# Attention's softmax sum in an audio tower: the second tree level moves from GpSimd to VectorE

## The reference, cut to what matters

```python
logits = jnp.einsum('avhd,bthd->abhvt', k, q) / math.sqrt(HEAD_DIM)   # a: 64 videos, v: 12 frames, h: 2 heads
weights = jax.nn.softmax(logits, axis=3)                              # over the 12 frames
attn = jnp.einsum('avhd,abhvt->abhtd', v, weights)
attn = attn.transpose(0, 1, 3, 2, 4).reshape(V, T, Nw, EMBED)
attn = attn.mean(axis=0)                                              # over the videos
o = attn @ Wo.T + bo
```

## Time and profile before

| | us |
|---|---|
| median of 3 runs | 2392.04 |
| lowest and highest | 2386.63, 2396.46 |
| the profiled execution's own time | 2387.96 |
| its span | 2386.1 |
| PE busy | 2052.9 (86%) |
| DVE busy | 1563.6 (66%) |
| ACT busy | 1079.6 (45%) |
| POOL busy | 769.3 (32%) |
| the 96 chunks of attention, in the span | about 1145 to 1635 |

### The profile page before, as it was taken

The page is one execution under the profiler, slowest core; times in us unless marked ns, Lnnn a source line. Parts: engine busy times, 40 slices in busy tenths (PEclk is TensorE's granted clock), DMA queues, the critical chain, the costliest instruction groups (busy, mean ns, idle before and its releaser), DMA issues. The chain is left out here.

```text
span 2386.1 us, 54761 instructions
## 1 busy us (share of the span) xinstructions
PE 2052.9 (86%) x20986; PEld 1812.3 (76%) x20986; DVE 1563.6 (66%) x3984; ACT 1079.6 (45%) x2700; POOL 769.3 (32%) x730
## 2 busy tenths in 40 slices
PE   6599989998726776786899999994999999999998
PEld 5497778786615676686677777773999999999998
DVE  4745665654743653556699999996666676676664
ACT  4433333422614453452666666662444444444443
POOL 0002222200055424520577777774121121121120
PEclk9899999999858897898999999997999999999999
DMA  7100100100311101100000000000000000000000
GB/s 180 37 1 12 15 11 12 15 1 2 111 42 35 30 20 35 36 16 1 3 3 3 3 3 3 3 3 1 8 8 7 13 7 7 13 7 7 13 7 14
DMA packets 80356, 44.52 MB, mean 19 GB/s; under 512 B 45800, under 2 KB 74024, under 8 KB 79752
## 3 DMA queue, kind: packets, MB, share of 16 engines
q1 hardware_dynamic: 74248, 29.53, 5.4%
q0 software_dynamic: 5888, 12.07, 1.9%
HBM read 27.20 MB, written 14.38 MB: 17 GB/s over the span
## 5 line engine op out<-in xcount | busy, mean ns | idle before, releaser
L2103 ACT ACTIVATE w<-banks,b 128x384 f32<-128x384 f32 (+1 forms) x512 | 259.5, 572 | 392.9 <-PE banks L2177 392.9
L2159 PE MATMUL banks<-w,w 128*128 128x128 f32 (+1 forms) x3072 | 364.1, 275 | 0.0
L2159 PEld LDWEIGHTS banks<-w,w 128*128 128x128 f32 (+1 forms) x3072 | 350.4, 189 | 9.1 <-issue 8.7
L1694 PE MATMUL banks<-qT,w 64*64 64x128 f32 x4608 | 272.2, 271 | 14.9 <-DVE eb L1597 12.3
L1702 PE MATMUL banks<-eb,w 64*64 64x128 f32 x4608 | 272.4, 271 | 0.7 <-DVE eb L1597 0.7
L1694 PEld LDWEIGHTS banks<-qT,w 64*64 64x64 f32 x4608 | 249.3, 133 | 29.8 <-DVE eb L1597 17.0
L2004 DVE SCALAR_TENSOR_TENSOR h<-banks,t_wt,h 128x128 f32 (+3 forms) x672 | 183.9, 343 | 115.1 <-PE banks L2159 112.4
L1702 PEld LDWEIGHTS banks<-eb,w 64*64 64x64 f32 x4608 | 249.2, 133 | 1.3 <-DVE eb L1597 1.1
L1237 POOL DMA_INDIRECT xg<-xs,rowu x184 | 179.2, 974 | 152.3 <-PE banks L1388 90.4
L1662 POOL TENSOR_TENSOR t<-eb 128x768 f32<-128x768 f32 x96 | 175.9, 1832 | 135.8 <-ACT eb L1642 123.7
L1597 DVE TENSOR_TENSOR eb<-eb,rd 128x1536 f32<-128x1536 f32 x96 | 211.7, 2205 | 1.6 <-ACT rd L1651 1.6
(11 more groups left out here) (309 smaller groups left out, 4354.4 us busy)
## 6 DMA issues: line engine op xcount, KB each, us to landing
out<-h SPq DMA_DIRECT2D x16, 320.0 KB
xs<-r_xl SPq DMA_DIRECT2D x16, 192.0 KB, 2.9
h<-in_xT SPq DMA_DIRECT2D x4, 750.0 KB, 15.0
h<-in_xT SPq DMA_DIRECT2D x4, 749.0 KB, 17.9
xg<-xs,rowu POOLq DMA_INDIRECT x184
xs<-r_xl SPq DMA_DIRECT2D x16, 128.0 KB
blocks<-NT SPq DMA_DIRECT2D x24, 48.0 KB, 1.9
D<-blocks SPq DMA_DIRECT2D x24, 48.0 KB, 2.0
```

Of the source, the lines that this page charges most:

```text
L1694: last = nc.tensor.matmul(lbanks(n)[place(n, hd), v, :], k.Kt[half(hd), v, :], qT[half(hd), n // NC % 2, (n % NC) * P:(n % NC + 1) * P], s ...
L2103: nc.scalar.activation(gb[u % 2][:, f, s * GW:s * GW + NFREE[s]], k.ps[:, order.bank(n), 0:NFREE[s]], ACT.Relu, bias=k.b1_1[:, 2 * e + f:2 ...
L2159: last = nc.tensor.matmul(k.psf[0:n, o:o + P], gb[u % 2][:, f, c * P:c * P + n], k.w2_1[:, 2 * e + f, :], start=(f == 0), stop=(f == 1))
```

## The change

`t1` gets a second buffer. POOL keeps only the first add, alternating between the buffers, and counts `tree` once a chunk. The second add moves to DVE, ahead of `den`, with a new semaphore `folded` on which DVE waits before it reads `t2`, and on which POOL waits before it writes a buffer of `t1` again.

```diff
-        t1 = sb("t1", [P, 6, P])
+        t1 = sb("t1", [P, 2, 6, P])
...
-        counted, logged = sem("ao_counted"), sem("logged")
+        counted, logged, folded = sem("ao_counted"), sem("logged"), sem("folded")
...
                     w = n - 2
                     if 0 <= w < NCH:
-                        dve.wait_ge(tree, 2 * w + 2)
+                        dve.wait_ge(tree, w + 1)
+                        nc.vector.tensor_tensor(t2[:], t1[:, w % 2, 0:3], t1[:, w % 2, 3:6], ALU.add).then_inc(folded, 1)
+                        dve.wait_ge(folded, w + 1)
                         if w >= 2:
                             dve.wait_ge(logged, w - 1)
                         nc.vector.tensor_reduce(den[:, w % 2, :], t2[:].rearrange("p v t -> p t v"), AX_X,
...
                 for n in range(NCH):
                     e = eb[:, n % 4]
                     pool.wait_ge(e_ready, 3 * n + 3)
-                    if n:
-                        pool.wait_ge(tree, 2 * n)
-                    nc.gpsimd.tensor_tensor(t1[:], e[:, 0:6], e[:, 6:12], ALU.add).then_inc(tree, 1)
-                    pool.wait_ge(tree, 2 * n + 1)
-                    if n:
-                        pool.wait_ge(summed, n)
-                    nc.gpsimd.tensor_tensor(t2[:], t1[:, 0:3], t1[:, 3:6], ALU.add).then_inc(tree, 1)
+                    if n >= 2:
+                        pool.wait_ge(folded, n - 1)
+                    nc.gpsimd.tensor_tensor(t1[:, n % 2], e[:, 0:6], e[:, 6:12], ALU.add).then_inc(tree, 1)
```

## The result

| | before | with the change |
|---|---|---|
| median, lowest, highest of 20 runs, us | 2391.8, 2382.9, 2409.3 | 2384.7, 2373.0, 2392.5 |
| ratio to before, 95% interval | | 0.9967 (0.9953 to 0.9982) |
| from the first maximum of attention to the first instruction behind it | 490.97 us | 484.67 us |

A forecast was written before the change was run, and what follows sets the result against it. PE and DVE are near full, with PE's own cycle as the floor. Saving 0.31 us a cycle, times 14, gives 4.3; the ends give 0.7; 5.0 off 2392.04 makes 2387.0 us, range 2378 to 2397.

The forecast's parts named there:

- floor of 29.23 us a cycle: PE alone could run six attention iterations in 29.23 us against 30.08, a ceiling near 12 us over 14 steady cycles.
- The fold: 0.55 and 0.03 of gap: The add moved to DVE takes 0.55 us plus 0.03 waiting for its semaphore: a slot of 0.58, bounds 0.47 and 0.70.
- The new wait behind ACT: 0.54: PE's turn of x waits 0.54 us for ACT's output copy, once a cycle; before, the wait for the multiply covered it.
- C: Third of six PE iterations in a cycle, with a turn of x; its first matmul waited for DVE's multiply before.
- The sum: 4.3 + 0.7: 0.31 us less a cycle, times 14, gives 4.3 us; both ends of attention give 0.7; together 5.0 us off.
- 0.1 us of slot costs 0.2 a cycle: Each 0.1 us more on the fold's DVE slot comes twice before den, so costs 0.2 us a cycle.
- The multiply's mean at 2.05 to 2.1: Sign that the forecast is right: DVE's multiply in attention averages 2.05 to 2.1 us.
- The walk's 0.5 and 0.8 us: Walking one cycle, the multiply stands still 0.5, 0.8, 0.5 and 0.8 us in the last four of six iterations.
- Rival 1, all 12 us: No new wait behind ACT appears, so all 12 us come back: 12.6 us off, 2379.4 us; chance 0.15.
- Rival 3: The fold starts after POOL's add and stands until it ends: 25 us more, 2417 us; chance 0.15.
- B: Second of six PE iterations in a cycle, plain; the fold was expected to start 0.47 us before POOL's add there.
- Without the second buffer POOL would wait for the fold: In attention, the bigger t1 is on no path and costs nothing; with one buffer POOL would wait for the fold.

The follow-up runs named there:

- experiment 3: The change with ACT's three normalisations moved ahead of the logarithm; attention stretch 478.24 us, 6.4 below the change, ratio 0.9934 to before.
- experiment 8: The change without the fold: POOL writes a token's six frames adjacent in t1, one DVE reduce sums them; stretch 476.83 and 476.93 us, ratio 0.9933 to before.
- experiment 9: The change with POOL's add cut to one token of 128, other sums left out; stretch 476.84 us, 7.8 below the change, ratio 0.9938 to before.
- experiment 4: The kernel before, with only ACT's normalisations moved ahead of the logarithm; stretch 490.98 us against 490.97 before, ratio 0.9998.
- experiment 5: Repeat runs of the change, 484.66 us, ratio 0.9989 to before, and of the change with ACT's normalisations ahead of the logarithm, 478.28 us, ratio 0.9944.
- experiment 6: The change with one DVE reduce of six frames in place of fold and den; stretch 497.14 us, 12.5 over the change, ratio 1.0025 to before.
- experiment 7: The change with one six-frame reduce for fold and den, and ACT's normalisations ahead of the logarithm; stretch 488.51 us, 3.8 over the change, ratio 1.0000.
- experiment 10: The change with the fold done twice, each with its wait; stretch 571.11 us, 86 over the change, ratio 1.0339 to before.
- experiment 2: The change with only one buffer for t1; stretch 484.93 us, 0.26 over the change, ratio 0.9976 to before.
- experiment 1: The kernel before with only the second buffer of t1, both adds left on POOL; stretch 488.67 us, 2.3 less than before, ratio 0.9992.

## Why the prediction was right, point by point

- *PE bounds, with a floor of 29.23 us a cycle.* Right. Experiments 3, 8 and 9 reach 29.22, 29.24 and 29.23 by three different ways and go no lower, though 9 frees 29 us of DVE.
- *The fold: 0.55 and 0.03 of gap.* 0.54 and 0.03 to 0.04. The Trainium skill's sentence ("VectorE: DVE Perf Modes", section "The DRAIN you can't avoid") that a semaphore costs nothing is about eight copies and does not fit these rows: a DVE instruction that waits for nothing starts 0.08 to 0.09 us before the record ahead ends (the maximum behind `den`, the fold behind `bn_stats`), and `den`, which waits for the fold's semaphore, 0.03 to 0.04 after it. No run has the fold and `den` without that semaphore.
- *The new wait behind ACT: 0.54.* 0.47 measured, in C and nowhere else. The 0.12 that I put between ACT's copy and the turn was an upper bound, and the trace has 0.06: the copy ends at 1300.72 and the turn starts at 1300.78. Experiments 3 and 4 show that ACT's order is its cause, and that the old wait covered it.
- *The sum: 4.3 + 0.7.* The cycle gave 0.39 and not 0.31, so 5.5 in 14 cycles; the other 0.8 of the 6.3 us is what remains for the ends, where 0.7 were an estimate. At the start it does not come as I had put it: `den` of the first chunk is 0.48 us earlier (7.74 us behind the first maximum, 8.22 before), but the first multiply stands beside POOL's next add and ends 13.57 us behind that maximum in both kernels; the gain comes in the iterations after it. The term that was mis-sized is the wait in C, by 0.07 us. That the measured medians and ratio came near (7.1 and 7.9 us) is in part luck, as experiment 5 shows.
- *0.1 us of slot costs 0.2 a cycle.* The cycle of experiment 6 fits it, at a slot 0.33 longer. It is no longer of use where DVE sets the cycle (experiments 7 and 10).
- *The multiply's mean at 2.05 to 2.1.* 2.057. The walk's 0.5 and 0.8 us are the times until POOL's add ends; the multiply itself grew by 0.33 in C and 0.65 in D, since it then ended 1.61 after that add and not 1.74.
- *Rival 1, all 12 us.* Not with this change; experiment 3 is what it would have taken.
- *Rival 3.* It did not occur, but its margin is real: in B the fold starts at 1297.55, 4.39 into it, and POOL's add at 1298.03, 0.48 later. Experiment 10 uses the margin up, and the fold stands as the rival said. What it adds to every iteration makes DVE the bound at the same time, so its 86 us are not the price of one late fold a cycle; the rival's 25 us stay untested.
- *"Without the second buffer POOL would wait for the fold".* It does, and no one waits for POOL: 0.26 us (experiment 2). The buffer by itself gave 2.3 us in the old form, which I had put at nothing (experiment 1); in the changed kernel it is worth those 0.26.
- *The ruler.* The range had to hold 10 us of spread between runs of one kernel. For so small an effect the stretch in the trace tells more than the time: three kernels that were profiled twice repeat it within 0.1 us.

## What to carry to other kernels

Where one engine is near full, take its own cycle from the starts of its iterations first: it is a ceiling that no cure of the others lifts, and here it was 12 us of a wait list that added up to 46. Then walk one cycle with the waits that remain, since the wait you remove often covers another one of nearly its size; that one may be cured by an order of instructions that was worth nothing before. Add up each engine's iteration again after every edit: two of these experiments made DVE the bound unnoticed, and a price worked out with PE as the bound no longer held. And before adding an instruction, ask what layout would let the next one do its work: the writer had the time to put the frames side by side, and the reader then needed no second step.

## What the runs showed of the hardware that I had not expected

- A reduce on DVE of six values to an output, 128 outputs, takes 1.48 us when the six lie 512 bytes apart in SBUF, and 0.93 when they are adjacent. Three values 512 bytes apart take 0.59, and twelve from PSUM 1.75; on the line through these two, six would take 0.98. So distance alone does not explain it, nor does POOL's add beside it, as all 96 take 1.46 to 1.53 us; why six are dear is open.
- POOL's add writes its 768 results 24 bytes apart as fast (1836 ns) as in rows (1821 ns).
- A DVE add of two SBUF inputs that begins after POOL's add has begun ends 0.42 us after it, whole: the Trainium skill's rule ("SBUF — State Buffer", section "SBUF: two separate sides") of a lock that is held to the instruction's end fits this too. One-input reduces were not held: `den` has a mean of 594 ns in the changed kernel, where in B it runs beside POOL's add (1298.13 beside 1298.03), and 594 ns in experiment 9, where POOL is nearly idle.
